# Attention probabilities in one tile per head pair with both key chunks side by side, and products in runs of eight heads

## The chip, the cores and the metric

The kernel runs on one core of one Trainium2 chip. The metric is device time in microseconds (us) of one launch. The core's engines are TensorE (matrix multiply, PE in the profile, its weight load PEld), VectorE (DVE), ScalarE (ACT), GpSimd (POOL) and SyncE (SP, which issues DMA copies here). They run in parallel, each with its own queue of instructions in program order, and wait for each other through semaphores.

## The reference

A small audio tower: a recurrent tokenizer, one layer of distance attention with eight heads, one mixture-of-experts layer. The input is (32, 4, 250): 32 sequences of 250 tokens. The part that the change touches is the attention:

```python
xn = _ln(x, ln_scale)
Q, K, V = (einsum('bse,hef->bhsf', xn, W) for W in (W_q, W_k, W_v))   # 8 heads of 64
sqdist = maximum(q2 + k2 - 2.0 * qk, 0.0)          # q2, k2: squared norms
scores = exp(-gamma * sqdist)                      # no softmax, no sum over keys
out = einsum('bhst,bhtf->bhsf', scores, V)         # (B, H, 250, 64)
return out.transpose(0, 2, 1, 3).reshape(B, S, H * E) @ W_o.T
```

The maximum with 0 is done after the exponential: for positive gamma the probability is capped at 1 from above (and, for a negative one, held at 1 from below).

## The kernel before

There are three stages: A (the tokenizer, to about 97 us), B (the attention, to about 540 us), C (the experts, to the end). Names as in the code: T = 125 tokens (half a sequence), L = 250, C = 500 (a pair of sequences), H = 8 heads, PAIRS = 16 pairs of sequences.

**Stage B** is a software pipeline over steps `p` = 0 to 17. Step p does the projections of pair p ("new"), the scores, caps and products of pair p-1 ("old") and the last products and the fold of pair p-2 ("old2"). Every step is cut into eight slots, v = 0 to 7, and each engine's queue is written out by hand slot by slot (`step_b`, one function for each engine).

*Scores.* Slot v belongs to sequence b = v // 4 of the pair and to the two heads 2v and 2v+1 (modulo 8). For each of two key chunks c of 125 keys TensorE makes one score tile n = 2v + c, [125 keys, 2 heads, 250 queries], with two matmuls of 500 columns (lines 1086 and 1088) into one of three banks, 5 + n % 3. Tile n waits until the Exp that last used its bank is done; the first tile of a step waits for all 16 Exps of the step before.

*Exp and cap.* ScalarE writes Exp of the tile into `prob[n % 8]` (line 539). VectorE caps it in place, one instruction for each head, since the cap depends on the head's gamma and is a per-partition scalar (line 784, `caps`):

```python
def caps(v, c):
    n = 2 * v + c
    dve.wait_ge(b_exp, 16 * (p - 1) + n + 1)
    for hh in range(2):
        part = prob[n % PROBS][:, hh, :]
```

With 8 tiles of [125, 2, 250] an Exp waits for the products of four slots before (`b_pv`).

*Products.* TensorE multiplies each head's probabilities with `u` (values already multiplied with the output weights) and accumulates over heads and keys in bank 1, for one sequence at a time (line 1062, `products`). One head and chunk is one matmul in the code and two in the profile, of 250 columns. The products of two slots are done in one go ("a run", 16 matmuls in the profile): those of slots v-2 and v-1 at the end of slot v = 2, 4, 6, and those of slots 6 and 7 in slot 0 of the next step. When a sequence's eight heads are in, ScalarE takes bank 1 to `y_att` (`evac_y`, line 532; in slot 4 and slot 0), and in slot 1 TensorE transposes both into bank 0 (`fold_b`, line 1070), from where VectorE adds them to the residual (lines 772, 775, slots 2 and 3).

*Projections of the next pair.* 16 units k, in slots 1 to 7 (3, 3, 2, 2, 2, 2, 2), interleaved with the score tiles. Each is two matmuls of 500 or 512 columns (lines 1110 and 1114), in banks 2 + k % 3. Units 0 to 7 give Q and K, of which only squared norms are wanted: ScalarE squares (line 553), GpSimd adds halves (line 405), VectorE reduces (line 794) two units later; GpSimd then makes `qkw` (lines 409, 412), which TensorE transposes in slot 5 (line 1145), and ScalarE (`rnd2`, line 577) and VectorE (line 825) make `s2` from it. Units 8, 10, 12, 14 ("G") are evacuated by ScalarE in two parts to `m1` (line 548), and VectorE subtracts (line 800, two instructions) into `m2`; projection k + 3 waits for that. Units 9, 11, 13, 15 are `u` (line 557). Projection k waits for the evacuation of k - 3.

*Tokens.* In slot 0 TensorE transposes the next normalised tokens (line 1043), which GpSimd finishes at the end of the step before (`b_scales`, `xn`, line 394); ScalarE and VectorE turn them into `s1` (lines 517, 521, 755).

*DMA.* SyncE copies halves of `m1` and rows of `s2` (its queue waits for `b_ev` and `b_s2`).

In step 16 there is no new pair, and stage C starts between the slots (`start_c`); step 17 has only the last products.

Of the kernel before, what the change touches and what calls it, by code (L numbers as in the profile page):

```python
# [7 lines left out]
ALU = mybir.AluOpType  # L8
ACT = mybir.ActivationFunctionType
AX = mybir.AxisListType  # L10
F32 = mybir.dt.float32
# [4 lines left out]
B, D_IN, L = 32, 4, 250  # L16
D = 64
H = 8
# [5 lines left out]
T = L // 2  # L24
PAIRS = B // 2
C = 2 * L
# [46 lines left out]
def build(nc, cst, xin, xparts, aw1, aw2, cw1, cw2, w24, wqT, wkT, wvT, woT, wq, wk, gam, lns,  # L73
          gw, gb, w1, b1, w2, b2, fg, fb, out):
    with ExitStack() as ctx:
# [58 lines left out]
        def phase(*tensors):  # L134
# [18 lines left out]
        m1, s2, u_sb, sq, sq2, prob, y_att = phase(  # L153
            ("m1_", 2, [128, H, C], F32R), ("s2_", 2, [S_ROWS, C], F32R), ("u", 2, [T, CH, H * D], F32), ("sq", 2, [T, H, D], F32),
            ("sq2_", 2, [T, H, D // 2], F32),
            ("prob", PROBS, [T, 2, L], F32), ("y_att", 2, [128, L], F32))
        relu_sb, gated, (y_moe,), (y_low,), (y_high,), (yt,), (stats2,), (yz,), (res,), wb = phase(
            ("relu", 3, [128, C], F32), ("gated", 8, [128, C], F32), ("y_moe", 1, [128, C], F32), ("y_low", 1, [128, C], F32),
            ("y_high", 1, [128, C], F32),
# [30 lines left out]
        def wait(eng, s, value):  # L190

            if not (isinstance(value, int) and value <= 0):
                eng.wait_ge(s, value)
# [286 lines left out]
        def _(act):  # L480
# [53 lines left out]
            def step_b(p, j, old2, old, new, ln):  # L534
                def exps(v, c):
                    n = 2 * v + c
                    act.wait_ge(b_sc, 16 * (p - 1) + n + 1)
                    wait(act, b_pv, 8 * (p - 1) + v - 3)
                    act.activation(prob[n % PROBS][:, :, :], bank[5 + n % 3][0:T, 0:C].rearrange("p (h l) -> p h l", h=2),  # L539
                                   ACT.Exp).then_inc(b_exp, 1)  # L540

                def unit(k):
                    src = bank[2 + k % 3]
                    act.wait_ge(b_pj, 16 * p + k + 1)
                    if is_g(k):
                        wait(act, b_sc, 16 * (p - 1))
                        for a in range(2):
                            last = act.activation(m1[j][64 * a:64 * a + 64, k - 8 + a, :],  # L548
                                                  src[64 * a:64 * a + 64, 0:C], ACT.Copy)
                        last.then_inc(b_ev, 1)  # L550
                    elif k < 8:
                        wait(act, b_sum, 8 * p + k - 1)
                        act.activation(sq[k % 2][:, :, :], src[0:T, :].rearrange("p (h d) -> p h d", h=H), ACT.Square)\  # L553
                            .then_inc(b_ev, 1)
                    else:
                        wait(act, b_pv, 8 * (p - 1))
                        act.activation(u_sb[j][:, (k - 8) // 2, :], src[0:T, :], ACT.Copy).then_inc(b_ev, 1)

                for v in range(8):
                    if new and v == 0 and not first_step(p):  # L560
                        round_b(p, j)
                    rest = list(units(v)) if new else []
                    for c in range(2):
                        if old:
                            exps(v, c)
                        if rest:
                            unit(rest.pop(0))
                    if v == 0 and old2:
                        evac_y(p - 2, 1)
                    if v == 4 and old:  # L570
                        evac_y(p - 1, 0)
                    for k in rest:
                        unit(k)
                    if new and v == 5:
                        act.wait_ge(b_qt, p + 1)
                        wait(act, b_s2, p)
                        act.activation(rnd2[64:S_ROWS, :], bank[0][64:S_ROWS, 0:C], ACT.Copy).then_inc(b_rnd2, 1)
                    if p == PAIRS:
                        start_c(v)
# [79 lines left out]
        def _(dve):  # L659
# [115 lines left out]
                    dve.tensor_tensor(rows, part, z2[:, :, :], ALU.add).then_inc(b_res, 1)  # L775

            def step_b(p, j, old2, old, new, ln):
                def caps(v, c):
                    n = 2 * v + c
                    dve.wait_ge(b_exp, 16 * (p - 1) + n + 1)  # L780
                    for hh in range(2):
                        h = (2 * v + hh) % H
                        part = prob[n % PROBS][:, hh, :]
                        last = dve.tensor_scalar(part, part, cap_hi[0:T, h:h + 1], cap_lo[0:T, h:h + 1],  # L784
                                                 ALU.min, ALU.max)
                    last.then_inc(b_cap, 1)

                def unit(k):
                    if 2 <= k < 10:
                        n = k - 2  # L790
                        if n == 0:
                            wait(dve, b_qkw, 2 * p)
                        dve.wait_ge(b_sum, 8 * p + n + 1)
                        dve.tensor_reduce(qk[:, n // 2, n % 2, :], sq2[n % 2][:, :, :], AX.X, ALU.add)\  # L794
                            .then_inc(b_red, 1)
                    if is_g(k):
                        dve.wait_ge(b_ev, 16 * p + k + 1)
                        for a in range(2):
                            rows, h = slice(64 * a, 64 * a + 64), k - 8 + a
                            last = dve.tensor_tensor(m2[j][0:64, h, :], bank[2 + k % 3][rows, 0:C],  # L800
                                                     f32(m1[j][rows, h, :]), ALU.subtract)
                        last.then_inc(b_gl, 1)

                if p == PAIRS - 1:
                    wait(dve, b_xn, PAIRS)
                    c_stats(0)
                    c_aggr(0)
                for v in range(8):
                    if new and v == 0 and not first_step(p):
                        stack_b(p, j)  # L810
                    rest = list(units(v)) if new else []
                    for c in range(2):
                        if old:
                            caps(v, c)
                        if old2 and v == 3 and c == 0:
                            residual(p - 2, 1)
                        if rest:
                            unit(rest.pop(0))
                    for k in rest:
                        unit(k)  # L820
                    if v == 2 and old2:
                        residual(p - 2, 0)
                    if new and v == 5:
                        dve.wait_ge(b_rnd2, p + 1)
                        dve.scalar_tensor_tensor(s2[j][64:S_ROWS, :], f32(rnd2[64:S_ROWS, :]),
                                                 c_sb[64:S_ROWS, C_MS2:C_MS2 + 1], bank[0][64:S_ROWS, 0:C],
                                                 ALU.mult, ALU.add).then_inc(b_s2, 1)
                    if ln and v == 0:
                        norm_stats(p + 1, b_ln)
                    if ln and v == 1:  # L830
                        norm_aggr(p + 1, b_ln)
                    if p == PAIRS:
                        start_c(v)
# [127 lines left out]
        def _(pe):  # L961
# [89 lines left out]
            def products(p, v, jj, hh):  # L1051

                b = v // 4
                if hh == 0:
                    pe.wait_ge(b_cap, 16 * p + 2 * v + 2)
                    if v == 0:
                        pe.wait_ge(b_ev, 16 * (p + 1))
                    if v % 4 == 0:
                        wait(pe, b_y, 2 * p + b)
                h = (2 * v + hh) % H  # L1060
                for c in range(2):
                    last = pe.matmul(bank[1][64 * c:64 * c + 64, 0:L], u_sb[jj][:, 2 * b + c, h * D:(h + 1) * D],  # L1062
                                     prob[(2 * v + c) % PROBS][:, hh, :], start=h == 0, stop=h == H - 1)
                if hh == 1:
                    last.then_inc(b_pv, 1)

# [7 lines left out]
            def step_b(p, j, old2, old, new, ln):  # L1074
# [43 lines left out]
                for v in range(8):  # L1118
# [9 lines left out]
                            unit(rest.pop(0))  # L1128
                    for k in rest:
                        unit(k)  # L1130
                    for n in (v - 2, v - 1) if v % 2 == 0 else ():
                        for hh in range(2):
                            if v == 0 and old2:
                                products(p - 2, n + 8, j, hh)
                            if v > 0 and old:
                                products(p - 1, n, o, hh)
                    if old2 and v == 1:
                        if new:
                            pe.wait_ge(b_s1, p + 1)
                        fold_b(p - 2)  # L1140
# [16 lines left out]

            def step_b_tail(p, j, old2, old, new, ln):
                if p == PAIRS + 1:
                    for n in (6, 7):  # L1160
                        for hh in range(2):
                            products(p - 2, n, j, hh)
                else:
                    step_b(p, j, old2, old, new, ln)
# [175 lines left out]
```

## Time and profile before

| | |
|---|---|
| median of 3 runs | 837.46 us (837.07 to 837.6) |
| the profiled execution | 838.8 us, span 837.0 us |
| TensorE | 764.6 us busy (91%), 5712 matmuls |
| VectorE | 697.4 us busy (83%), 1793 instructions |
| ScalarE | 540.2 us busy (65%) |
| GpSimd | 459.6 us busy (55%) |
| caps, line 784 | 512 instructions 125x250, 232.7 us busy |
| products, line 1062 | 1024 matmuls 64x250, 127.0 us busy |
| Exp, line 539 | 256 instructions 125x500, 148.7 us busy |

The span is the time from the first to the last instruction in the profile of one execution. Busy time of matmuls is the union of overlapping records: a matmul of 500 columns is recorded with 0.39 us, but the next starts 0.23 us later. Records on VectorE and ScalarE overlap a little too, so start-to-start distances in a timeline say what an instruction costs its queue, and the record's length says when its result is there.

### The profile page before, as it was taken

The numbers are of one execution on the slowest core, as the hardware profiler recorded it, in microseconds if no ns is written. First come the engines' busy times: TensorE is split into PE (matmuls) and PEld (weight loads), VectorE is DVE, ScalarE is ACT, GpSimd is POOL, SyncE is SP. The second block draws the span as 40 slices with busy tenths as digits, with TensorE's granted clock in tenths as the row PEclk, the third lists the DMA queues.
The fourth block names the chain that finished last, engine by engine and source line by source line (L and its number), as shares of the span: only waits on it lengthen the run. The fifth ranks groups of instructions, "written<-read, shape, count | busy, mean of one in ns | idle before, by whom it ended". The sixth has DMA issues, their size and how long they took to land.

```text
span 837.0 us, 17065 instructions
## 1 busy us (share of the span) xinstructions
PE 764.6 (91%) x5712; PEld 449.4 (54%) x5712; DVE 697.4 (83%) x1793; ACT 540.2 (65%) x1058; POOL 459.6 (55%) x628
## 2 busy tenths in 40 slices
PE   2999879999999999999999998899999999999993
PEld 1343446666666666666666665445555555455441
DVE  3676669999999999999999997788888888888861
ACT  1565678887878878887788877444555555446442
POOL 8741254534445354544445441256777777777776
PEclk9999989999999999999999999999999999999997
DMA  6300022111221112211121112000000000000000
GB/s 159 115 2 2 1 50 52 34 32 38 50 52 26 39 39 52 51 27 38 41 51 39 38 28 51 1 3 1 8 14 8 8 7 8 11 12 7 8 7 19
DMA packets 22862, 25.72 MB, mean 31 GB/s; under 512 B 12888, under 2 KB 21720, under 8 KB 22648
## 3 DMA queue, kind: packets, MB, share of 16 engines
q1 hardware_dynamic: 21608, 23.57, 12.1%
q10 hardware_dynamic: 1168, 1.07, 0.6%
q8 instruction: 47, 0.77, 0.4%
q14 instruction: 39, 0.32, 0.1%
HBM read 5.30 MB, written 2.43 MB: 9 GB/s over the span
## 4 chain that ended last, share of the span: by engine, by line
PE 44%; DVE 44%; issue 5%; ACT 3%; POOL 2%; ACTq 1%; DMA 1%; POOLq 0%; DVEq 0%
DVE prob L784 16%; DVE m L800 9%; PE bank L1198 7%; PE bank L1177 6%; PE bank L1062 6%; PE bank L990 6%; PE bank L1110 5%; DVE gated L915 4%; PE bank L1086 3%; PE bank L1088 2%; DVE qk L794 2%; DVE top L897 2%; PE bank L1231 2%; PE bank L980 2%; DVE top L901 1%
## 5 line engine op out<-in xcount | busy, mean ns | idle before, releaser
L784 DVE TENSOR_SCALAR prob<-prob,cap_hi,cap_lo 125x250 f32<-125x250 f32 x512 | 232.7, 502 | 23.2 <-ACT prob L539 20.6
L405 POOL TENSOR_TENSOR sq<-sq 125x256 f32<-125x256 f32 x128 | 96.2, 758 | 171.3 <-ACT sq L553 126.7
L539 ACT ACTIVATE prob<-bank 125x500 f32<-125x500 f32 x256 | 148.7, 591 | 37.3 <-PE bank L1088 34.2
L1198 PE MATMUL bank<-gated,w_sb 64*64 64x500 f32 x1024 | 164.5, 585 | 0.0
L1177 PE MATMUL bank<-cs,w_sb 64*64 64x500 f32 x1024 | 161.7, 580 | 1.8 <-DVE gated L915 1.6
L442 POOL TENSOR_TENSOR gated<-relu,wb 128x500 f32<-128x500 f32 x96 | 120.0, 1251 | 71.2 <-ACT relu L633 71.1
L915 DVE SCALAR_TENSOR_TENSOR gated<-bank,nb,wb 128x500 f32<-128x500 f32 x160 | 115.6, 732 | 41.9 <-PE bank L1177 41.7
L1062 PE MATMUL bank<-prob,u 125*64 125x250 f32 x1024 | 127.0, 385 | 2.2 <-DVE prob L784 0.8
L633 ACT ACTIVATE relu<-bank,b_sb 128x500 f32<-128x500 f32 x96 | 64.7, 674 | 98.1 <-PE bank L1177 98.1
L1086 PE MATMUL bank<-m,s 128*125 128x500 f32 x256 | 111.3, 435 | 8.2 <-issue 6.2
L1088 PE MATMUL bank<-m,s 112*125 112x500 f32 x256 | 101.2, 395 | 0.0
L1062 PEld LDWEIGHTS bank<-prob,u 125*64 125x64 f32 x1024 | 66.9, 137 | 57.2 <-issue 17.6
L553 ACT ACTIVATE sq<-bank 125x512 f32<-125x512 f32 x128 | 76.6, 600 | 20.3 <-POOL sq L405 17.3
L800 DVE TENSOR_TENSOR m<-bank,m 64x500 fp32r<-64x500 f32 x128 | 86.3, 674 | 3.9 <-ACT m L548 1.6
L1177 PEld LDWEIGHTS bank<-cs,w_sb 64*64 64x64 f32 x1024 | 57.5, 133 | 56.6 <-issue 47.1
L1110 PE MATMUL bank<-wqku_hi,s 128*125 128x512 f32 x192 | 77.7, 405 | 6.2 <-DVE m L800 3.6
L1110 PE MATMUL bank<-wqku_lo,s 128*125 128x512 f32 x192 | 76.9, 401 | 0.0
L1198 PEld LDWEIGHTS bank<-gated,w_sb 64*64 64x64 f32 x1024 | 53.7, 133 | 41.4 <-issue 32.0
L548 ACT ACTIVATE m<-bank 64x500 fp32r<-64x500 f32 x128 | 74.1, 579 | 0.8
L1086 PEld LDWEIGHTS bank<-m,s 128*125 128x125 f32 x256 | 48.1, 188 | 41.3 <-issue 32.4
L990 PE MATMUL bank<-st_a,w_sb 64*64 64x500 f32 x224 | 58.5, 595 | 0.0
L990 PE MATMUL bank<-st_b,w_sb 64*64 64x500 f32 x224 | 58.0, 595 | 0.0
(169 smaller groups left out, 1347.7 us busy)
## 6 DMA issues: line engine op xcount, KB each, us to landing
m<-m SPq DMA_DIRECT2D x128, 125.0 KB, 2.3
out<-res SPq DMA_DIRECT2D x16, 125.0 KB
xa<-xparts SPq DMA_DIRECT2D x4, 281.2 KB
w_sb<-in_w SPq DMA_DIRECT2D x1, 1024.0 KB
xw<-xparts SPq DMA_DIRECT2D x4, 140.6 KB
w_sb<-in_w SPq DMA_DIRECT2D x1, 512.0 KB
m<-s SPq DMA_DIRECT2D x32, 15.6 KB
xparts<-x_part SPq DMA_DIRECT2D x1, 375.0 KB, 4.8
```

The costliest lines, as they stand in the source:

```text
L442: gp.tensor_tensor(gated[g % 8][:, :], relu_sb[n % 3][:, :], wb[q % 2][:, :], ALU.mult).then_inc(c_gatep, 1)
L539: act.activation(prob[n % PROBS][:, :, :], bank[5 + n % 3][0:T, 0:C].rearrange("p (h l) -> p h l", h=2), ACT.Exp).then_inc(b_exp, 1)
L784: last = dve.tensor_scalar(part, part, cap_hi[0:T, h:h + 1], cap_lo[0:T, h:h + 1], ALU.min, ALU.max)
L800: last = dve.tensor_tensor(m2[j][0:64, h, :], bank[2 + k % 3][rows, 0:C], f32(m1[j][rows, h, :]), ALU.subtract)
L915: dve.scalar_tensor_tensor(gated[g % 8][:, :], up_bank(g)[:, 0:C], nb1[:, g:g + 1], wb[q % 2][:, :], ALU.max, ALU.mult).then_inc(c_gated, 1)
L990: last = pe.matmul(dst[cols, 0:C].rearrange("p (b l) -> p b l", b=2), w24_sb[rows, 0, :], src[rows, :, 0:L], start=False, stop=True)
L1062: last = pe.matmul(bank[1][64 * c:64 * c + 64, 0:L], u_sb[jj][:, 2 * b + c, h * D:(h + 1) * D], prob[(2 * v + c) % PROBS][:, hh, :], start ...
L1086: pe.matmul(ps, s1[o][:, cols], m1[o][:, 2 * hp:2 * hp + 2, b * L:(b + 1) * L], start=True, stop=False)
L1088: pe.matmul(ps, s2[o][:, cols], m2[o][:, 2 * hp:2 * hp + 2, b * L:(b + 1) * L], start=False, stop=True).then_inc(b_sc, 1)
L1110: last = pe.matmul(dst[0:T, :], s1[j][:, c * T:(c + 1) * T], w[:, q, :], start=first, stop=not first)
L1177: last = pe.matmul(up_bank(g)[cols, 0:C], w1_sb[rows, g, cols], cs1[q % 3][rows, :], start=True, stop=True)
L1198: last = pe.matmul(y[cols, 0:C], w2_sb[rows, g, :], gated[g % 8][rows, :], start=g == 1 and rows is HI, stop=v == 7, skip_group_check=True)
```

## The change

`prob` becomes eight tiles of [125, 2 heads, 2 chunks, 250]. Exp of chunk c writes the part [:, :, c, :], in rows of 250 with a gap. One cap covers both chunks of a head, 500 elements next to each other, and waits for both Exps of the slot; on VectorE it stands behind the projection unit instead of ahead of it. An Exp now waits for the products of the eighth slot before. Products are done for four slots (eight heads, one sequence; 32 matmuls in the profile) in a row, in slot 4 and in slot 0 of the next step. `evac_y` moves to slots 5 and 1, `fold_b` to slot 2.

```diff
-            ("prob", PROBS, [T, 2, L], F32), ("y_att", 2, [128, L], F32))
+            ("prob", PROBS, [T, 2, 2, L], F32), ("y_att", 2, [128, L], F32))
@@ ScalarE, step_b
-                    wait(act, b_pv, 8 * (p - 1) + v - 3)
-                    act.activation(prob[n % PROBS][:, :, :], bank[5 + n % 3][0:T, 0:C].rearrange("p (h l) -> p h l", h=2),
+                    wait(act, b_pv, 8 * (p - 1) + v - 7)
+                    act.activation(prob[v % PROBS][:, :, c, :], bank[5 + n % 3][0:T, 0:C].rearrange("p (h l) -> p h l", h=2),
                                    ACT.Exp).then_inc(b_exp, 1)
...
-                    if v == 0 and old2:
+                    if v == 1 and old2:
                         evac_y(p - 2, 1)
-                    if v == 4 and old:
+                    if v == 5 and old:
                         evac_y(p - 1, 0)
@@ VectorE, step_b
-                def caps(v, c):
-                    n = 2 * v + c
-                    dve.wait_ge(b_exp, 16 * (p - 1) + n + 1)
-                    for hh in range(2):
-                        h = (2 * v + hh) % H
-                        part = prob[n % PROBS][:, hh, :]
-                        last = dve.tensor_scalar(part, part, cap_hi[0:T, h:h + 1], cap_lo[0:T, h:h + 1],
-                                                 ALU.min, ALU.max)
-                    last.then_inc(b_cap, 1)
+                def caps(v, hh):
+                    h = (2 * v + hh) % H
+                    dve.wait_ge(b_exp, 16 * (p - 1) + 2 * v + 2)
+                    part = prob[v % PROBS][:, hh, :, :]
+                    dve.tensor_scalar(part, part, cap_hi[0:T, h:h + 1], cap_lo[0:T, h:h + 1], ALU.min, ALU.max)\
+                        .then_inc(b_cap, 1)
...
                     for c in range(2):
-                        if old:
-                            caps(v, c)
                         if old2 and v == 3 and c == 0:
                             residual(p - 2, 1)
                         if rest:
                             unit(rest.pop(0))
+                        if old:
+                            caps(v, c)
@@ TensorE, products and step_b
-                                     prob[(2 * v + c) % PROBS][:, hh, :], start=h == 0, stop=h == H - 1)
+                                     prob[v % PROBS][:, hh, c, :], start=h == 0, stop=h == H - 1)
...
-                    for n in (v - 2, v - 1) if v % 2 == 0 else ():
+                    for n in range(v - 4, v) if v % 4 == 0 else ():
                         for hh in range(2):
...
-                    if old2 and v == 1:
+                    if old2 and v == 2:
                         if new:
                             pe.wait_ge(b_s1, p + 1)
                         fold_b(p - 2)
@@ TensorE, step_b_tail
-                    for n in (6, 7):
+                    for n in (4, 5, 6, 7):
```

## Rows read from the trace of the kernel before

**Rows 1.** Busy time of each engine in one of seven like stretches (stage B)

```profile
...
core 0: us, PE busy (x) PEld busy (x) DVE busy (x) ACT busy (x) POOL busy (x), PEclk, DMA share, GB/s
...
300.00:350.00 50.00, 47.09 (x265) 31.86 (x266) 47.54 (x120) 40.73 (x79) 22.08 (x37) 1.00 0.17 39
...
```

**Rows 2.** Chain of waits, one step: start us, us, what

```profile
...
303.36 1.07 PE bank L1062 x8
...
305.55 0.23 PE bank L1086
...
306.02 0.94 PE bank L1110 x4
306.95 0.44 PE bank L1070 x4
...
312.22 0.60 ACT prob L539
...
312.84 0.73 DVE prob L784 x2
...
329.87 1.07 PE bank L1062 x8
...
```

**Rows 3.** The instructions of line 784: duration ns least/median/most

```profile
...
L784 DVE TENSOR_SCALAR prob<-prob,cap_hi,cap_lo x512: 380/405/1539, 118.8 to 539.1; 125x250 f32<-125x250 f32 x171
...
```

**Rows 4.** Groups of instructions on VectorE: busy us, mean ns

```profile
...
L800 DVE TENSOR_TENSOR m<-bank,m 64x500 fp32r<-64x500 f32 x128 | 86.3, 674 | 3.9 <-ACT m L548 1.6
...
L825 DVE SCALAR_TENSOR_TENSOR s<-rnd,c_sb,bank 48x500 fp32r<-48x500 f32 x16 | 11.9, 742 | 1.1 <-ACT rnd L577 0.6
...
L697 DVE TENSOR_SCALAR cap_hi<-cap_lo 128x8 f32<-128x8 f32 x1 | 0.2, 171 | 0.0
...
```

**Rows 5.** Timeline of TensorE, around the products of slot 2: start, us, instruction

```profile
...
309.30 0.39 PE L1110 MATMUL bank<-wqku_lo,s 128*125 128x512 f32 x1
309.61 1.91 PE L1062 MATMUL bank<-prob,u 125*64 125x250 f32 x16
311.45 0.49 PE L1086 MATMUL bank<-m,s 128*125 128x500 f32 x1
311.79 0.40 PE L1088 MATMUL bank<-m,s 112*125 112x500 f32 x1
...
```

**Rows 6.** Timeline of ScalarE, slots 1 and 5

```profile
...
304.48 0.38 ACT L532 ACTIVATE y_att<-bank 128x250 f32<-128x250 f32 x1 [1.08 <-PE bank L1062]
...
317.94 0.59 ACT L539 ACTIVATE prob<-bank 125x500 f32<-125x500 f32 x1 [0.26 <-PE bank L1088]
318.42 1.16 ACT L548 ACTIVATE m<-bank 64x500 fp32r<-64x500 f32 x2
319.61 0.59 ACT L539 ACTIVATE prob<-bank 125x500 f32<-125x500 f32 x1
320.09 0.59 ACT L557 ACTIVATE u<-bank 125x512 f32<-125x512 f32 x1
320.92 0.58 ACT L577 ACTIVATE rnd<-bank 48x500 fp32r<-48x500 f32 x1 [0.24 <-PE bank L1145]
321.53 0.59 ACT L539 ACTIVATE prob<-bank 125x500 f32<-125x500 f32 x1
...
```

**Rows 7.** Timeline of TensorE, idle stretches outside the steady steps

```profile
...
113.62 0.50 PE L1110 MATMUL bank<-wqku_hi,s 128*125 128x512 f32 x1 [1.89 <-DVE m L800]
...
115.91 1.09 PE L1043 MATMUL bank<-c_sb,xn 125*128 125x125 f32 x4 [1.57 <-POOL xn L394]
...
518.54 0.62 PE L1215 MATMUL bank<-c_sb,cxn 125*128 125x125 f32 x4 [2.10 <-ACT cxn L605]
...
527.54 0.78 PE L1086 MATMUL bank<-m,s 128*125 128x500 f32 x1 [1.92 <-ACT prob L539]
...
528.67 3.00 PE L1062 MATMUL bank<-prob,u 125*64 125x250 f32 x16
...
```

**Rows 8.** Timeline of GpSimd, the end of slot 7

```profile
...
325.25 1.30 POOL L394 TENSOR_TENSOR xn<-z,lns_sb 125x512 f32<-125x512 f32 x1
...
```

## The prediction

> **What bounds the kernel now.** I read busy time by stretch first, then the chain of waits, then the timelines of one steady step. From 300 to 350 us, as in the six other stretches of 50 us from 150 to 500, TensorE is busy 47.1 of 50 us and VectorE 47.5, the granted clock at 1.00 [rows 1]: both are near their limit. The chain of waits shows how they share it. It passes products at 303.36 and again at 329.87, so a step takes 26.51 us; in between it runs on TensorE up to 312.2 (slots 1 to 3), crosses one Exp, and from 312.84 stays on VectorE until the products of the next slot 0 [rows 2]. So slots 3 to 7 are VectorE's, slots 0 to 3 TensorE's. ScalarE and GpSimd have time left over the step as a whole; whether ScalarE has it in each slot is the question of this change.
>
> **The caps.** 32 instructions of 250 elements a step become 16 of 500. Today's shortest takes 380 ns, the median 405 [rows 3]. Does it handle one element a cycle or two? A tensor_scalar of 8 elements with immediates takes 171, a two-input operation of 500 elements 674, one of 500 with a per-partition scalar 742 [rows 4]. So 503 ns pay for 492 elements (1.02 ns each), and a per-partition scalar costs some 68. A cap at that rate would need 171+247+68 = 486 ns; it takes 380. It therefore pays about half as much per element, and 250 more cost 0.13 us. Start to start a cap takes 0.33 us (two end after 0.73, less 0.405); the wide one 0.46 (bounds 0.33, if all were fixed cost, and 0.59). VectorE is relieved of 32x0.33 - 16x0.46 = 3.2 us a step (1.1 to 5.3). The Trainium skill (VectorE: DVE Perf Modes, The perf-mode tier table) also gives fp32 tensor_scalar within SBUF twice the rate of a two-input one; at the single rate the relief would be the 1.1.
>
> Two thirds of the chain lay on VectorE, so it goes to whoever is next, and that decides.
>
> **The products.** The same 64 matmuls a step come in two runs of 32 (slots 4 and 0) in place of four of 16 (slots 0, 2, 4, 6). Sixteen take 1.84 us (309.61 to 311.45), 32 so 3.68. Going in costs 0.08 (0.31 where 0.23 is usual), coming out 0.11 (0.34) [rows 2, 5]. TensorE's work today: 16 score tiles 7.3, 16 projections 7.4, four runs 8.1, fold and two sets of transposes 1.4 (0.44 to 0.5 each), together 24.2 us; two changes less make it 23.8. By TensorE alone the step would gain 2.7.
>
> **The waits.** An Exp now waits for products of the pair before, long done: free. A cap waits for both chunks' Exp and stands behind the projection unit; products of slot 3 are wanted only 2.76 us into the long run, so that is covered. The y evacuations (slots 1 and 5), fold_b (slot 2) and its residuals move along behind the runs; the DMA copies keep their place in SP's queue. Not covered is this: the scores of slot 5 can't start before the long run of slot 4 ends, ScalarE runs dry during it, and then has three slots of evacuations to do before the scores of slot 0, whose first tile waits for all 16 Exps. TensorE used to do 16 products inside just that time. Now it does them in the runs, when ScalarE has nothing to do.
>
> ScalarE's stretch [rows 6]: Exp 0.48 (317.94 to 318.42), the two-part G evacuation 1.19 (to 319.61), Exp 0.48, u some 0.48 (the 320.09 start to the next, less the 0.24 waited for), rnd2 0.61 (320.92 to 321.53). From the first Exp of slot 5 to the end of the last of slot 7: five Exps 2.40, the sixth 0.62 with its signal, three G 3.57, two u 0.96, rnd2 0.61, and newly y, 0.27 (its 0.38 less the 0.11 by which records on ScalarE overlap): 8.43. With gaps I take 8.5 us.
>
> The loop from the end of the run in slot 0: slots 1 to 4 on TensorE, 8 score tiles of 0.457, 10 projections of 0.466, fold 0.44, coming out 0.11: 8.87. Into the run 0.08, run 3.68. First scores of slot 5 0.57, and 0.19 to the Exp (311.79+0.23 to 312.22). ScalarE 8.5. To the scores of slot 0 0.1, two tiles 1.0, into the run 0.08, run 3.68. Sum 26.75 us, against 26.51: **0.24 us a step longer**. VectorE's G subtractions and caps, three times 1.4+0.9, fit beside ScalarE there. From step 2 to step 16 that is 14 loops: +3.4 us. The first step with scores has one run less before its slot 4 (-0.5), and the last, with eight caps in a row ahead of its final products, gains about 6 pairs x 0.2, of which I take 1.0 (bounds -2.5 and +1). Without more: +1.9.
>
> **The clock.** TensorE now works 23.8 of 26.75 us, and its 3 idle us lie together: projection 15 waits for the subtraction of G 12 (1.7), the tokens for GpSimd's last steps (0.3), the scores for the last Exp (0.7), with 0.5 of work between each. The trace has three stretches like that [rows 7]. After idle 2.10 (to 518.54) matmuls keep their pace. After 1.89, one projection and 1.57 more (to 115.91) four transposes take 1.09 instead of 0.62, and after 1.92 (to 527.54) a score matmul takes 0.78 instead of 0.49 and 16 products 3.00 instead of 1.91 [rows 5]: the lower level of the clock, 1.2 instead of 2.4 GHz. That second fall lies over one score tile and a run: 0.6+1.1 = 1.7 us lost. In the new loop what follows the idle time is the scores of slot 0 and the long run, both on the path. Two of three fell, but my longest idle piece is shorter than in each of them, so I take 5 of 14 steps (bounds none and all): 5x1.7 = +8.5 us, bounds 0 and 24.
>
> The Trainium skill (TensorE: Matmul & The Clock Gate, Why this matters for your kernels) wants no long idle gaps between bursts, but sets its mark above the gaps that these rows show before a fall. By that rule the clock would hold, which is the first rival.
>
> **Sum.** 837.46+3.4-0.5-1.0+8.5 = 847.9, so **848 us**. The profiled execution took 838.8 (span 837.0); the terms are differences within it, added to the runs' median, 837.46, which is 1.3 lower.
>
> **Rivals.**
> 1. The clock holds and only the loop counts: 837.5+1.9 = 839.4 us, range 837 to 842. For it: it is at 1.00 all through the stage today. Against: the idle time, now 2.3 us, is longer and lies together.
> 2. The other side: the relief of VectorE decides. The same loop with the runs split as today sums to 8.87+2.03+1.92+0.76+8.23+0.4+1.1+1.92 = 25.2 us (0.4: ScalarE's wait for the run of slot 6), which VectorE's 26.51 hides. If the long runs cost nothing on top, because ScalarE catches up behind them, 14x1.3 = 18 us go: 819. It begins to decide where ScalarE's stretch is under 8.25 us with the clock up; each 0.1 us is 1.4 us of time. For it: 26.75 and 26.51 are close for a sum of 25 pieces. Against: each piece is a row, and both waits stand in the code.
> 3. The wide cap and GpSimd hold each other up. A cap that starts beside GpSimd's xn takes 1.54 us instead of 0.38, as long as that runs (1.30) [rows 3, 8]. Square (ScalarE), half sum (GpSimd) and reduction (VectorE) reach projection 9 with under 0.3 us to spare by my count, and a cap now holds 0.13 us longer and stands between the reductions. At 0.5 us a step lost: +7, so 846 with the clock up and 855 with the falls. The Trainium skill (SBUF — State Buffer, SBUF: two separate sides) calls the port that both use an exclusive lock for a whole instruction; the row agrees.
>
> **Chances.** The loop with a falling clock 0.42 (842 to 862, by 3 to 14 falls); the clock holds 0.21; the faster rival 0.18 (819 to 835); port and reductions 0.12; small errors that cancel and leave no difference 0.07. Under 0.2% (1.7 us) a measurement of this kernel can't tell from no change. Slower by more: 0.42, 0.12, 0.11 of the second case and 0.03 of the last: 0.68. Same 0.14, faster 0.18. The range leaves out the better part of the faster rival and a little above: 832 to 862; the likeliest case's own is 842 to 862.
>
> **What the changed profile would show.** 256 caps 125x500, shortest about 510 ns; VectorE busy 85% of a step; no caps on the chain in slots 3 to 7, which instead alternates between 32 products and ScalarE's Exps and G evacuations. ScalarE idle for 1.5 to 3 us before the first Exp of slots 1 and 5. TensorE waiting over 1 us before projection 15 for the G subtraction, and again for an Exp before the scores of slot 0, and no more for qkw. A step of 26.7 us where the granted clock is 1.0, over 28 where it falls. I am wrong if a step is under 26.3 us, if ScalarE idles inside slots 5 to 7, or if the caps take 640 ns.

## The result, and the profile after

The changed kernel takes 855.23 us (median of 4 runs, 850.07 to 856.22) against 837.53 of the kernel before on the same chip: a ratio of 1.0198, 95% interval 1.0164 to 1.0233. It is slower, by 17.7 us. The profiled execution is the quickest of the changed kernel's, 850.07 us with a mean granted clock of 0.969; the other runs lie at 0.960 to 0.963.

The page of the changed kernel: engines, shares of the chain that ended last, and the group of the caps (line 782 is the cap, was 784; 1059 the products, was 1062; 797 the subtraction of G, was 800).

```profile
PE 763.0 (90%) x5712; PEld 460.3 (54%) x5712; DVE 620.4 (73%) x1537; ACT 532.4 (63%) x1058; POOL 462.8 (55%) x628
PE 63%; DVE 18%; issue 10%; ACT 6%; POOL 2%; ACTq 1%; DMA 1%; POOLq 0%; SPq 0%; DVEq 0%
L782 DVE TENSOR_SCALAR prob<-prob,cap_hi,cap_lo 125x500 f32<-125x500 f32 x256 | 149.5, 611 | 71.8 <-ACT prob L539 69.6
```

The caps are busy 149.5 us instead of 232.7, VectorE 620.4 instead of 697.4.

The caps are not all alike. Two undisturbed wide caps take 0.99 us together, and these two, in GpSimd's way with its half sums (line 405), 1.54:

```profile
309.73 1.54 DVE L782 TENSOR_SCALAR prob<-prob,cap_hi,cap_lo 125x500 f32<-125x500 f32 x2 [4.24 <-ACT prob L539]
310.26 0.73 POOL L405 TENSOR_TENSOR sq<-sq 125x256 f32<-125x256 f32 x1 [0.23 <-ACT sq L553]
```

Over the changed kernel the 90 caps that overlap a half sum are on average 0.23 us longer than the shortest, the other 166 some 0.03. In the kernel before, 14 caps beside `xn` are 1.15 longer, 165 beside half sums 0.23, and the rest again some 0.03.

VectorE is off the chain: its share fell from 44% to 18%, TensorE's rose from 44% to 63%. The next view is busy time by stretch, one step at full clock and then most of one in which the clock fell (columns as in [rows 1]).

```profile
327.70:354.20 26.50, 24.22 (x141) 17.27 (x140) 20.19 (x46) 20.85 (x42) 12.71 (x20) 1.00 0.18 41
354.20:380.70 26.50, 25.44 (x140) 17.78 (x138) 18.88 (x44) 19.42 (x39) 11.33 (x20) 0.94 0.18 40
```

VectorE is busy 20.2 of 26.5 us, where it was at 95% [rows 1]. Yet the step has the length that it had. The chain of the changed kernel, from the long run of slot 4 to that of slot 0, says why. It answers to [rows 2], where this stretch belonged to VectorE.

```profile
316.44 3.52 PE bank L1059 x32
319.96 0.42 PE bank L1083
...
320.67 0.44 issue
321.13 0.45 ACT m L548
...
325.37 0.59 ACT m L548
...
326.67 0.69 DVE m L797
327.40 0.74 PE bank L1107 x2
328.13 0.43 PE bank L1040 x4
328.56 0.73 issue
329.29 0.46 PE bank L1083
```

The run ends, two score matmuls follow, and from 320.67 to 327.40 the chain lies on ScalarE's queue and what hangs on it, then on the short pieces in front of the scores of slot 0. No cap is on it. ScalarE's timeline shows the two ends of its stretch, and the wait ahead of it and behind it (to be held against [rows 6]).

```profile
320.65 0.59 ACT L539 ACTIVATE prob<-bank 125x500 f32<-125x500 f32 x1 [1.54 <-PE bank L1085]
...
328.61 0.59 ACT L539 ACTIVATE prob<-bank 125x500 f32<-125x500 f32 x1
...
334.66 0.59 ACT L539 ACTIVATE prob<-bank 125x500 f32<-125x500 f32 x1 [3.10 <-PE bank L1085]
```

From 320.65 to the end of the Exp at 329.20 it works without a break: 8.55 us. The last Exp releases the scores 0.09 us later, at 329.29. ScalarE stands idle 1.54 us before this stretch and 3.10 before the first Exp of slot 1. TensorE's timeline around the same place, at full clock and then a step later:

```profile
327.40 0.50 PE L1107 MATMUL bank<-wqku_hi,s 128*125 128x512 f32 x1 [1.56 <-DVE m L797]
...
329.29 0.46 PE L1083 MATMUL bank<-m,s 128*125 128x500 f32 x1 [0.73 <-issue]
...
330.37 3.59 PE L1059 MATMUL bank<-prob,u 125*64 125x250 f32 x32
333.89 0.50 PE L1083 MATMUL bank<-m,s 128*125 128x500 f32 x1
...
353.89 0.50 PE L1107 MATMUL bank<-wqku_hi,s 128*125 128x512 f32 x1 [1.55 <-DVE m L797]
...
355.78 0.75 PE L1083 MATMUL bank<-m,s 128*125 128x500 f32 x1 [0.73 <-issue]
...
357.71 4.27 PE L1059 MATMUL bank<-prob,u 125*64 125x250 f32 x32
361.91 0.49 PE L1083 MATMUL bank<-m,s 128*125 128x500 f32 x1
```

Both times TensorE idles 1.55 us, works 0.8 (two projection matmuls, four transposes), idles 0.73 and begins the scores. The wait called "issue" is one for which the profile names no cause. I take it for the one for the last Exp, which in each of these steps ends about 0.1 us before the scores start; e9 below tests that. The first time, scores and run take 4.60 us (329.29 to 333.89). The second time they take 6.13 (355.78 to 361.91): the granted clock went from its upper to its lower level, 2.4 to 1.2 GHz, and came back inside the run. One fall costs 1.5 us. Between the starts of the scores of slot 0, the steps are 26.45 to 26.56 us without a fall and 27.96 to 28.08 with one (29.59 once). In this execution 5 of the 14 steps have one.

Step 16, the last with scores, is where the rest went. TensorE's timeline:

```profile
521.16 4.46 PE L1059 MATMUL bank<-prob,u 125*64 125x250 f32 x32
...
534.90 0.78 PE L1083 MATMUL bank<-m,s 128*125 128x500 f32 x1 [4.29 <-ACT prob L539]
...
536.03 5.55 PE L1059 MATMUL bank<-prob,u 125*64 125x250 f32 x32
...
547.64 4.87 PE L1059 MATMUL bank<-prob,u 125*64 125x250 f32 x32
```

There is no projection in this step to fill TensorE. It waits 4.29 us for an Exp where it waited 1.92 [rows 7], and all three runs of 32 lie partly at the lower clock (3.59 at the full one). In the profiled executions:

| stretch | before | after | difference |
|---|---|---|---|
| to the scores of slot 0, step 2 | 142.17 | 139.22 | -3.0 |
| 14 steps to those of step 16 | 371.28 | 380.16 | +8.9 |
| step 16, to the first matmuls of stage C after it | 27.05 | 33.06 | +6.0 |
| the rest of 838.8 and 850.07 | 298.3 | 297.6 | -0.7 |

### The profile page after: what moved, and what is told of

Read it like the earlier page. It is cut to its first block, busy times and chain, and to the rows that moved or that the text cites. A ratio compares the mean times of both kernels' runs of the same rounds, so it can differ in the third digit from the quotient of the medians.

```text
span 848.3 us, 16801 instructions
## 1 busy us (share of the span) xinstructions
PE 763.0 (90%) x5712; PEld 460.3 (54%) x5712; DVE 620.4 (73%) x1537; ACT 532.4 (63%) x1058; POOL 462.8 (55%) x628
## 4 chain that ended last, share of the span: by engine, by line
PE 63%; DVE 18%; issue 10%; ACT 6%; POOL 2%; ACTq 1%; DMA 1%; POOLq 0%; SPq 0%; DVEq 0%
PE bank L1059 14%; PE bank L1107 9%; PE bank L1195 7%; PE bank L1174 6%; PE bank L1083 6%; PE bank L987 6%; PE bank L1085 5%; DVE gated L912 4%; ACT m L548 3%; DVE m L797 3%; DVE top L894 2%; PE bank L1228 2%; PE bank L977 2%; DVE top L898 1%; PE bank L1220 1%
## 5 line engine op out<-in xcount | busy, mean ns | idle before, releaser
L782 DVE TENSOR_SCALAR prob<-prob,cap_hi,cap_lo 125x500 f32<-125x500 f32 x256 | 149.5, 611 | 71.8 <-ACT prob L539 69.6
L539 ACT ACTIVATE prob<-bank 125x500 f32<-125x500 f32 x256 | 150.6, 597 | 78.3 <-PE bank L1085 76.3
L1059 PE MATMUL bank<-prob,u 125*64 125x250 f32 x1024 | 124.2, 399 | 0.0
L1107 PE MATMUL bank<-wqku_hi,s 128*125 128x512 f32 x192 | 80.8, 421 | 29.2 <-DVE m L797 26.0
L1085 PE MATMUL bank<-m,s 112*125 112x500 f32 x256 | 103.2, 403 | 0.0
L1059 PEld LDWEIGHTS bank<-prob,u 125*64 125x64 f32 x1024 | 74.8, 146 | 48.6 <-issue 15.2
L553 ACT ACTIVATE sq<-bank 125x512 f32<-125x512 f32 x128 | 78.4, 613 | 15.7 <-POOL sq L405 11.1
L1107 PEld LDWEIGHTS bank<-wqku_hi,s 128*125 128x125 f32 x192 | 36.5, 190 | 50.9 <-DVE m L797 39.3
```

What stands on the lines that cost most here:

```text
L539: act.activation(prob[v % PROBS][:, :, c, :], bank[5 + n % 3][0:T, 0:C].rearrange("p (h l) -> p h l", h=2), ACT.Exp).then_inc(b_exp, 1)
L1085: pe.matmul(ps, s2[o][:, cols], m2[o][:, 2 * hp:2 * hp + 2, b * L:(b + 1) * L], start=False, stop=True).then_inc(b_sc, 1)
L1107: last = pe.matmul(dst[0:T, :], s1[j][:, c * T:(c + 1) * T], w[:, q, :], start=first, stop=not first)
```

## The experiments

**e1: wide caps, short runs.** The changed kernel with the runs of the kernel before. It separates the two parts of the change.

```diff
-                    for n in range(v - 4, v) if v % 4 == 0 else ():
+                    for n in (v - 2, v - 1) if v % 2 == 0 else ():
```

and `evac_y` back in slots 0 and 4, `fold_b` in slot 1, the tail back to slots 6 and 7.

> Wide tiles and wide caps stay; the products go back to four runs of 16 (slots 2, 4, 6 and 0), y evacuations and fold back with them. If the long runs are what costs (a ScalarE stretch that starts only behind a run), a steady step takes 25.2 us instead of 26.5, TensorE never idles over 1 us in it and the granted clock there is 1.00: 837.5 - 14 x 1.3 = 819 us, 814 to 825. If the wide cap itself is the cost (it and GpSimd hold each other up), the time stays at 850 or more.

Measured: 820.49 us, ratio 0.9799 (0.9779 to 0.9818), a step of 25.27 us. The chain of one step, its run in slot 6 and its end, and below it the busy time of the step:

```profile
312.44 1.84 PE bank L1059 x16
...
316.84 0.48 issue
317.32 0.46 PE bank L1083
```

```profile
292.07:317.32 25.25, 24.77 (x141) 16.81 (x141) 20.71 (x46) 21.31 (x42) 12.70 (x20) 1.00 0.19 43
```

The step is TensorE's but for 0.48 us before the scores of slot 0. The relief of VectorE is worth 17 us as long as the runs are short. (The caps stand behind the projection unit here, as in the change; no run tells that order apart from the width.) So the whole loss, and as much again, is the long runs'.

**e2: narrow caps, long runs.** The other part alone, on the kernel before. It needs 16 narrow tiles, so that an Exp need not wait inside the run.

```diff
-PROBS = 8
+PROBS = 16
-                    wait(act, b_pv, 8 * (p - 1) + v - 3)
+                    wait(act, b_pv, 8 * (p - 1) + v - 7)
-                    for n in (v - 2, v - 1) if v % 2 == 0 else ():
+                    for n in range(v - 4, v) if v % 4 == 0 else ():
```

and `evac_y`, `fold_b` and the tail moved as in the change.

> The other half alone: 250-element caps, two for each tile, as before (16 narrow tiles, so the same memory and the same waits of an Exp), with the products in two runs of 32. If the loop through the long runs decides, VectorE takes ScalarE's place in slots 5 to 7 (three times 1.4 us of subtraction and four caps of 0.33, s2 0.7, about 1 us of waiting for GpSimd: near 10 us against ScalarE's 8.5), so a step takes about 28 us before any fall of the clock: 860 to 880 us. If the long runs cost nothing and the wide caps are to blame, it takes 838.

Measured: 853.04 us, ratio 1.0189 (1.0169 to 1.0209), steps of 26.5 to 26.9 us and, with a fall of the clock, 27.8 to 28.1. That is faster than any of my figures. I had put VectorE's slots 5 to 7 one behind the other onto the long run. The chain shows another road around it:

```profile
323.79 0.73 DVE prob L784 x2
324.52 0.34 DVE qk L794
...
324.93 0.41 POOL qkw L409
...
330.71 1.29 POOL xn L394
...
332.05 0.65 PE bank L1043 x4
```

Caps and reductions alternate on VectorE, `qkw` comes late, and GpSimd, which does everything for the next tokens behind it, brings `xn` late to TensorE. The caps of slots 5 to 7 have slack. The wide caps take this path away (in the changed kernel neither `qkw` nor `xn` holds TensorE up in the steady steps), but ScalarE's is as long.

| medians, us | runs of 16 | runs of 32 |
|---|---|---|
| narrow caps | 837.5 | 853.0 |
| wide caps | 820.5 | 855.2 |

With long runs the cap's width hardly shows in the time.

**e3: matmuls into the idle time.** The changed kernel, with six matmuls of 500 columns ahead of projection 15 in slot 7, into a bank whose content has been read and is overwritten before its next use. They add work and change no value.

```diff
+                        if new and old and v == 7 and c == 1:
+                            pe.wait_ge(b_s2, p + 1)
+                            for _ in range(6):
+                                pe.matmul(bank[0][:, 0:C], s1[o][:, 0:128], m1[o][:, 0, :], start=True, stop=True)
```

> The changed kernel with six extra score-like matmuls of 500 columns into bank 0, ahead of projection 15, where TensorE waits 1.5 us for the G subtraction; their result is overwritten unread. They do no work that is wanted; they only keep TensorE busy. If the falls of the clock are what the changed kernel loses in its steady steps, they go (granted clock 1.00 from 140 to 515 us), every step takes 26.5 us and the time is 855 less some eight falls of 1.6 us: 840 to 846. If the time is lost elsewhere, it stays at 855 or gets longer by what the extra matmuls take.

Measured: 838.08 us, ratio 1.0008 (0.9994 to 1.0022). All 14 steps take 26.50 us (139.97 to 510.93, so 370.96) at a granted clock of 1.00. TensorE's timeline:

```profile
321.85 1.52 PE L1127 MATMUL bank<-m,s 128*128 128x500 f32 x6
323.56 0.50 PE L1107 MATMUL bank<-wqku_hi,s 128*125 128x512 f32 x1 [0.19 <-DVE m L797]
...
325.45 0.46 PE L1083 MATMUL bank<-m,s 128*125 128x500 f32 x1 [0.72 <-issue]
...
326.54 3.59 PE L1059 MATMUL bank<-prob,u 125*64 125x250 f32 x32
```

The idle 1.56 us are filled, the loop is as long as before, and 17 us come back. In the 14 like steps the clock was the whole difference between the changed kernel and the one before (370.96 against 371.28 us). Outside them two differences nearly cancel: the scores of step 2 start 2.2 us sooner than before, and step 16 takes 1.8 longer. Step 16 is shorter too (28.86 us against 33.06), though nothing was put into it: it begins at the full clock (its first run takes 3.59 instead of 4.46).

**e4: short runs in step 16 alone.**

```diff
+            def runs(v, new):
+                if new or v == 0:
+                    return range(v - 4, v) if v % 4 == 0 else ()
+                return (v - 2, v - 1) if v % 2 == 0 else ()
```

> The changed kernel, with runs of 16 in step 16 alone (slots 2, 4, 6 and the tail), where no new pair is projected and stage C starts; all steady steps keep the long runs. If the 33.1 us of that step (27.1 before) come from the long runs, during which ScalarE and VectorE get nothing and the clock falls between them, it goes back to 27 to 29 us and the time to 849 to 852. If it is something else in that step, the time stays at 855.

Measured: 850.53 us, ratio 1.0145 (1.0115 to 1.0174). Step 16 takes 28.5 us instead of 33.1, nearly as in e1 (494.51 to 522.91, 28.4); so 4.6 of the 6.0 us there are the long runs'. The median is 4.7 below the changed kernel's. The profiled execution (853.2 us, clock 0.962) has a fall in 9 of its 14 steps, and they take 386.1 us.

**e5 and e6: one long run at a time.** Both from e1; e5 has the long run in slot 4 and keeps slots 6 and 0 short, e6 has it in slot 0 only.

```diff
+            RUNS = {4: (0, 1, 2, 3), 6: (4, 5), 0: (-2, -1)}        (e5)
+            RUNS = {2: (0, 1), 4: (2, 3), 0: (-4, -3, -2, -1)}      (e6)
-                    for n in (v - 2, v - 1) if v % 2 == 0 else ():
+                    for n in RUNS.get(v, ()):
```

> As e1 (wide caps, y evacuations and fold where they were), but one of the two long runs back: 32 products in slot 4, 16 in slots 6 and 0. If only what empties TensorE beside ScalarE's stretch of slots 5 to 7 costs, this long run is harmless: its 16 moved products come from slot 2 and stay ahead of the scores of slot 5 either way. One change of kind less a step, 0.19 us: step 25.1 us, clock 1.00, 818 us (815 to 821). If every long run costs, because ScalarE runs dry in it, half of the 1.2 us a step between e1 and the changed kernel comes back: 829 or more.

> As e1, but the other long run back: 16 products in slots 2 and 4, 32 in slot 0, nothing in slot 6. If the 16 products that left slot 6 are what costs, this is nearly the whole loss: a step of 26.4 us without a fall (26.5 of the changed kernel, one change of kind more, the y evacuation out of ScalarE's stretch), TensorE waiting 1.5 us before projection 15, falls of the clock as in the changed kernel, 842 to 853 us. If both long runs share the cost, it comes out like e5, near 830.

Measured: e5 816.5 us, ratio 0.9734 (0.9709 to 0.9759), a step of 24.87; e6 850.53 us, ratio 1.0149 (1.0128 to 1.017), steps of 26.5 to 26.6 and 27.7 to 28.2 with a fall (8 of 14). TensorE's waits in e6 between 150 and 500 us (in total, times, longest):

```profile
PE bank L1109 <- DVE m L797: 16.6, 13, 1.3
PE bank L1040 <- POOL xn L394: 4.6, 13, 0.4
```

The long run of slot 4 does no harm in the like steps: e5's step is 0.4 us shorter than e1's. One run less explains nearly all of that: two runs of 16 take 3.68 us and one of 32 takes 3.52, going in costs 0.08 and coming out 0.1. The forecast of 0.19 had left out the 0.16. In step 16, where no projection fills TensorE, the long run of slot 4 does cost: that step takes 30.2 us (488.54 to 518.77) against e1's 28.4. What costs in the like steps is that the 16 products of slots 4 and 5 leave slot 6, where they filled the time in which TensorE waits for others, and stand in slot 0. That their place in slot 0 does harm of its own, beside leaving slot 6 empty, is not shown: no run has one without the other.

**e7 and e8: the order in slot 7.** From e5: ScalarE does both Exps of slot 7 ahead of its evacuations of G 14 and u 15 (e7), and VectorE also the caps of slot 7 ahead of the subtraction of G 14 (e8).

```diff
-                        if rest:
+                        if rest and not (old and v == 7):
                             unit(rest.pop(0))
```

and, on VectorE, in e8 alone:

```diff
+                        if old and v == 7:
+                            caps(v, c)
-                        if rest:
+                        if rest and not (old and v == 7):
                             unit(rest.pop(0))
-                        if old:
+                        if old and v < 7:
                             caps(v, c)
```

> As e5, and in slot 7 ScalarE does both Exps before the evacuations of G 14 and u 15. In e1 TensorE's queue is the whole chain but for 0.49 us before the scores of slot 0, where it waits for the last Exp, which stands behind G 14. If that is so, the wait goes and a step takes 24.7 us: 14 x 0.4 less than e5, 812 us (809 to 815). If G 14, now later, holds up something that TensorE needs as soon, or VectorE or GpSimd are late by then, it equals e5.

> As e7, and in slot 7 VectorE too does its two caps before the subtraction of G 14. In e7 the caps of slot 7 stand behind that subtraction, which waits for the later evacuation, and TensorE waits 1.18 us for them inside the run of slot 0. If this is the whole of e7's loss, the wait goes, TensorE's queue is the chain without a gap and a step takes 24.4 us: 14 x 1.2 less than e7's 828, so 811 us (808 to 814). If the later G 14 holds up something else too, it stays above 816.

Measured: e7 828.29 us, ratio 0.9882 (0.9863 to 0.9902), 11.8 us slower than e5 and 16 over the forecast. The timeline of VectorE and TensorE:

```profile
294.94 1.36 DVE L797 TENSOR_TENSOR m<-bank,m 64x500 fp32r<-64x500 f32 x2 [1.08 <-ACT m L548]
...
296.34 0.99 DVE L782 TENSOR_SCALAR prob<-prob,cap_hi,cap_lo 125x500 f32<-125x500 f32 x2
...
297.38 1.06 PE L1059 MATMUL bank<-prob,u 125*64 125x250 f32 x8 [1.18 <-DVE prob L782]
```

TensorE's waits for the caps in e7 between 150 and 500 us (in total, times, longest):

```profile
PE bank L1059 <- DVE prob L782: 16.6, 13, 1.3
```

The scores of slot 0 start earlier, but VectorE's queue has the subtraction ahead of the caps of slot 7. The subtraction now waits 1.08 us for a G evacuated later, the caps wait behind it, and the products behind the caps. I had moved one engine's order and left the other's. With both moved, e8 takes 806.59 us, ratio 0.9629 (0.9608 to 0.9651): the shortest of all, 3.7% faster than the kernel before. Its chain is TensorE's without a gap, 24.12 us a step (its long run in slot 4, the short ones in slots 6 and 0 and the transposes of the tokens among others):

```profile
295.86 3.52 PE bank L1061 x32
...
303.92 1.84 PE bank L1061 x16
...
307.79 0.43 PE bank L1042 x4
```

**e9: the change as it is, with e8's order in slot 7.**

> The changed kernel with both long runs, and the order of e8 in slot 7 (both Exps, then G 14, u 15; both caps, then the subtraction). By the loop, ScalarE's stretch up to the last Exp is shorter by G 14, 1.19 us; the next in line is GpSimd's xn (ready about 0.8 us before the scores of slot 0 start now), so a step takes 25.7 us without a fall, TensorE is idle 0.7 us less and the clock falls less often: 14 x 0.8 and some falls off 855 us, 835 to 845. If the loop does not run through the last Exp, the time stays at 855.

Measured: 842.78 us, ratio 1.0053 (1.0026 to 1.0079). Steps take 25.8 us without a fall and 27.4 with one, 7 of each. TensorE's timeline, in a step of each sort:

```profile
302.18 0.50 PE L1109 MATMUL bank<-wqku_hi,s 128*125 128x512 f32 x1 [1.56 <-DVE m L797]
...
303.35 0.68 PE L1085 MATMUL bank<-m,s 128*125 128x500 f32 x1
...
305.21 3.98 PE L1061 MATMUL bank<-prob,u 125*64 125x250 f32 x28
...
355.33 0.49 PE L1109 MATMUL bank<-wqku_hi,s 128*125 128x512 f32 x1 [1.56 <-DVE m L797]
...
356.46 0.50 PE L1085 MATMUL bank<-m,s 128*125 128x500 f32 x1
```

The second wait (0.73 us) is gone and the loop is 0.7 shorter, as it should be if ScalarE's stretch set its end. The wait of 1.56 ahead of projection 15 stays, and alone it is enough for the clock to fall in half of the steps; they are the first seven of the 14, one after another. With both long runs this order in slot 7 does not make up for the empty slot 6.

## Why the prediction was right

848 us were forecast, slower by 1.3%, with the falling clock as the likeliest case; 855 were measured, inside the range and inside that case's own. Point by point:

- **The cap's price: right, the relief too small.** The shortest wide cap takes 509 ns (510 forecast), and undisturbed caps follow each other after 0.45 to 0.46 us. But VectorE's busy time fell by 5.2 us a step (232.7 less 149.5, over 16), at the upper bound of 1.1 to 5.3, not 3.2. The mean over the shortest explains the rest: a narrow pair takes 0.73 undisturbed, 0.365 a cap, against a mean of 232.7/512 = 0.455; a wide pair 0.99, 0.495, against 149.5/256 = 0.584. That is 0.09 us a cap at either width, and there are half as many. The average hides where it is lost: in the caps that run beside GpSimd, as the section on the result shows, so a part of rival 3 is true. So VectorE is busy 76% of a step, not 85%. As it had left the chain, this moved nothing in the sum.
- **The loop: right in kind, its term mis-sized.** ScalarE's stretch is 8.55 us (8.5), TensorE waits 1.56 and 0.73 (1.7 and 0.7 forecast), and the 0.3 for the tokens between them isn't there. A run of 32, though, takes 3.52 us from start to start, not twice 1.84: 16 matmuls more add 1.68, so 0.16 of the 1.84 comes once a run, and doubling counted it twice. Two runs, 0.3 us: the loop is 26.50, not 26.75, as e3 shows without any fall. The term of +3.4 us was 0 (14 steps take 370.96 us in e3, 371.28 in the kernel before).
- **The clock: right in kind, too small for the usual run.** 5 of 14 steps at 1.7 us were forecast. The profiled execution has 5, one of them double, for 9.3 us together; the other runs, at a lower mean clock, must have more, as e4's (9 of 14 at 0.962). If the 5.2 us between the profiled execution and the median are all further falls, the term of 8.5 us should have been some 14; that is an estimate. e3 shows the clock by an intervention: the stretch of 1.56 us filled, no fall in the 14 steps, 17 us back, some 4 of them in step 16. The Trainium skill (TensorE: Matmul & The Clock Gate, Why this matters for your kernels) sets its mark for idle gaps above those of these rows. By that the clock would have held; the traces disagree, since it fell after 1.56 and 0.73 us, and in e9 after 1.56 alone. Nor is it a matter of the longest gap alone: in e7 TensorE waits 1.2 to 1.3 us inside the products in every step, and none of the 14 shows a fall; in e6 it waits 1.2 to 1.3 and then 0.4, and 8 of 14 do.
- **The last step: wrong in sign.** I took -1.0 for caps that go faster, with +1 as the upper bound; it cost 6.0. I had looked at the products behind the last caps and not at what the long run leaves before them: TensorE with nothing to do for 4.29 us, and the lower clock over the run that follows. By e4, 4.6 us of it are the long runs'; the other 1.4, which e1 also has, stay with wide caps and short runs (its run behind the wait takes 3.60 where it was 3.00 [rows 7]), and I didn't follow them further.
- **The first step: -3.0 instead of -0.5.** In the kernel before, TensorE's matmuls ran at the lower level here from 115.9 us [rows 7] to 121 us (so the clock was not at 1.00 all through the stage, as the first rival has it); in the profiled execution of the changed one the idle pieces were 0.98 and 1.31 us instead of 1.89 and 1.57, and it stayed up. The terms that were off, -3.4, +7 and -2.5, nearly cancel, so the closeness of 848 to the profiled 850.07 is partly luck; the direction isn't.
- **The rivals.** Had the clock held, the time would be 839.4 by my sum; e3, where it holds, takes 838.1. The faster rival gave 819 for the loop with short runs, which is e1's 820.5: the sum was good, and the long runs keep it from happening. The third, the wide cap and GpSimd on the reductions' path, isn't seen on the path: the two do hold each other up, but projection 9 waits for nothing. e2 shows how near it is: with narrow caps and long runs the step's chain runs through it.

## What to carry to other kernels

Short work that is ready at any time, as these products are, is the filler of the slots in which an engine waits for others: collect it into long runs only where that leaves no such slot empty (here slot 4 in the like steps, not slot 0), whatever each change of kind saves. When the relief of one engine doesn't show, look at what the edit took out of the stretch that sets the end, and move the order on all engines of that stretch together (e7 against e8: 22 us). And count idle stretches of TensorE twice: for themselves, and for the lower clock over the work behind them.

## What was unexpected of the hardware

- TensorE's granted clock fell to its lower level after a single idle stretch of 1.56 us (e9), and after shorter ones close together: 1.2 to 1.3 and 0.4 us (e6), or 0.6, 1.1 and 0.7 (e2). It did so in some steps and not in others with the same instructions and the same waits (7 of 14 in e9, 8 in e6, 7 in e2, 5 in the changed kernel). It didn't in any of the 14 steps after 1.0 and 0.4 us (the kernel before) or 1.3 alone (e7). A fall costs 1.5 us if the work behind it is on the path. Six matmuls, 1.52 us of them, in the idle stretch kept it up throughout.
- Products 64x250 add 0.105 us a matmul from start to start (1.84 for 16, 3.52 for 32), so 0.16 of each run is fixed, and going in and coming out cost 0.08 and 0.1 besides.
- A cap of 500 elements costs VectorE 0.46 us from start to start where one of 250 costs 0.33; the mean cap is 0.09 us above the undisturbed one at either width, nearly all of it in the caps that overlap GpSimd's half sums and, in the kernel before, its `xn`.
